# Base product of an adaptive FFN layer with LoRA experts: Strassen's seven block products over pairs of rows, in two passes over the contraction

## The reference

```python
y      = einsum('bct,bcd->bdt', x, w_cond[idx])         # 128x128 matrix per row, picked by idx
base   = einsum('bnd,od->bno', y, W_base) + b_base      # W_base 2048 x 2048
probs  = softmax(einsum('bnd,ed->bne', y, W_gate))      # 8 experts
route  = weights of the two largest probs, divided by their sum
h      = einsum('bnd,erd->bner', y, A)                  # 8 experts x rank 16 = 128 features
delta  = einsum('bner,eor->bno', h * route, B)
out    = x + base + delta * 1.0
```

## Time and profile before

| | |
|---|---|
| time, median of 3 runs | 1686.07 us (1685.47 to 1686.70) |
| the profiled execution | 1686.61 us, its span 1684.7 us |
| busy share of the span | PE 98%, DVE 49%, ACT 15%, POOL 13% |
| mean granted TensorE clock | 0.992 of 2.4 GHz |
| DRAM traffic | 89.49 MB, mean 53 GB/s; 228 GB/s in the first of 40 slices |
| 128x512 matmuls | 5952 of the base product, 384 of the expert part |

### The profile page before, as it was taken

How to read it: one execution, slowest core, us unless ns; L and a number is a source line. 1 busy time by engine, 2 the same in 40 slices (tenths; PEclk the granted TensorE clock), 3 DMA queues, 4 the chain that set the end, 5 groups by cost and what they waited for, 6 DMA issues and landing times.

```text
span 1684.7 us, 27043 instructions
## 1 busy us (share of the span) xinstructions
PE 1645.8 (98%) x10563; PEld 893.3 (53%) x10563; DVE 827.8 (49%) x1801; ACT 247.7 (15%) x416; POOL 223.6 (13%) x132
## 2 busy tenths in 40 slices
PE   5899999999999999999999999999999999999998
PEld 5785555455555455555545555554555554555553
DVE  5866554444545454454445444545445444544452
ACT  5661111001011101011110101110001111010110
POOL 2652111100111110111111011111011111101110
PEclk8999999999999999999999999999999999999999
DMA  6341110111110111111011111101111101111100
GB/s 228 126 177 59 46 52 19 51 45 45 51 45 28 42 51 45 45 45 51 24 46 45 45 51 45 39 31 51 45 45 51 45 25 45 45 51 45 45 25 25
DMA packets 32111, 89.49 MB, mean 53 GB/s; under 512 B 3386, under 2 KB 8506, under 8 KB 25946
## 3 DMA queue, kind: packets, MB, share of 16 engines
q1 hardware_dynamic: 32090, 89.21, 14.5%
HBM read 55.64 MB, written 33.55 MB: 53 GB/s over the span
## 4 chain that ended last, share of the span: by engine, by line
PE 95%; DVE 2%; issue 1%; ACT 1%; DMA 0%; SPq 0%; DVEq 0%; POOL 0%; ACTq 0%; POOLq 0%
PE acc L732 26%; PE acc L731 26%; PE acc L733 26%; PE h_ps L733 2%; PE h_ps L731 2%; PE h_ps L732 2%; PE tr L731 2%; PE delta L731 2%; PE tr L732 2%; PE tr L733 2%; PE delta L733 2%; PE delta L732 2%; PE tr L784 1%; DVE WT L504 0%; DMA x_even<-in_x_dram 0%
## 5 line engine op out<-in xcount | busy, mean ns | idle before, releaser
L732 PE MATMUL acc<-WT,y_parts 128*128 128x512 f16 (+2 forms) x2240 | 799.6, 361 | 0.0
L731 PE MATMUL acc<-WT,y_parts 128*128 128x512 f16 (+2 forms) x2240 | 799.3, 361 | 0.0
L733 PE MATMUL acc<-WT,y_parts 128*128 128x512 f16 (+2 forms) x2240 | 799.3, 361 | 0.0
L733 PEld LDWEIGHTS acc<-WT,y_parts 128*128 128x128 f16 x2240 | 219.8, 98 | 234.1
L731 PEld LDWEIGHTS acc<-WT,y_parts 128*128 128x128 f16 x2240 | 219.8, 98 | 219.1
L732 PEld LDWEIGHTS acc<-WT,y_parts 128*128 128x128 f16 x2240 | 219.8, 98 | 217.8
L504 DVE SCALAR_TENSOR_TENSOR y_parts<-tr,y_parts 128x512 f16<-128x512 f32 x126 | 86.9, 691 | 238.3 <-ACT y_parts L352 237.7
L592 DVE SCALAR_TENSOR_TENSOR scaled_acc<-acc,y_inv,inv_w 128x512 f32<-128x512 f32 x128 | 95.8, 749 | 189.2 <-PE delta L733 182.8
L352 ACT ACTIVATE y_parts<-tr 128x512 f16<-128x512 f32 x126 | 75.1, 597 | 502.0 <-PE tr L733 501.9
L299 POOL TENSOR_TENSOR wait_taker<-amax,ident 128x2 f32<-128x2 f32 x32 | 6.3, 197 | 947.4 <-DVE amax L483 947.4
L476 DVE TENSOR_SCALAR clamped<-amax_all 128x2 f32<-128x2 f32 x32 | 5.4, 170 | 210.9 <-POOL amax_all L300 210.9
(11 more groups left out here) (175 smaller groups left out, 1393.5 us busy)
## 6 DMA issues: line engine op xcount, KB each, us to landing
x_even<-in_x_dram SPq DMA_DIRECT2D x16, 1024.0 KB, 4.8
x_odd<-in_x_dram SPq DMA_DIRECT2D x16, 1024.0 KB, 4.8
out_dram<-x_even SPq DMA_DIRECT2D x64, 256.0 KB, 2.5
out_dram<-x_odd SPq DMA_DIRECT2D x64, 256.0 KB, 2.5
x_odd<-in_L_ffn_W_base_dram SPq DMA_DIRECT2D x4, 1024.0 KB, 5.0
bias<-in_L_ffn_W_base_dram SPq DMA_DIRECT2D x4, 1024.0 KB, 4.8
spare<-in_L_ffn_W_base_dram SPq DMA_DIRECT2D x4, 1024.0 KB, 4.9
x_parts<-in_L_ffn_W_base_dram SPq DMA_DIRECT2D x3, 1024.0 KB, 4.7
```

The lines of the kernel that those rows point to most:

```text
L731: nc.tensor.matmul(dst, lhs[0], rhs[0], start=start, stop=False)
L732: nc.tensor.matmul(dst, lhs[0], rhs[1], start=False, stop=False)
L733: return nc.tensor.matmul(dst, lhs[1], rhs[0], start=False, stop=stop)
```

## The change

Rows are taken in pairs. With A the outputs of `cond` for the two rows (two rows by two halves of a piece of the contraction) and B the matching blocks of `W_base` (two halves of the contraction piece by two blocks of 512 outputs), four blocks of the result of 128x512 are made from seven block products in place of eight. Sums of A (S1 to S4), of B (T1 to T4) and of the results are needed for it.

- **Two passes.** The contraction of 2048 is cut into two halves of 1024. Steps 0 to 15 (first pass) take the 16 pairs over the first half, steps 16 to 31 over the second. A step makes 8 tiles of 128x512 (j or c and s below: two rows by four groups of outputs). The first pass adds residual and bias and stores each tile to `part_dram`; the second loads it again, adds its own half and the expert part, and stores to `out`.
- **W twice.** `TT` holds the seven B-combinations of one half, split (112 KB of each partition). It is built before step 0 and again, for the other half, between steps 15 and 16, each time in 8 units of two 128x1024 blocks of rows.
- **Features.** `make_features` sums into `BH` in each step; the first pass stores its half of h to `h_dram`, the second adds it. Routing and expert part are done in the second pass only, for both rows together.
- **Results.** ACT copies the partial products that are needed twice (`copy_p`), DVE makes tile and row scale (`finish`), POOL adds it to the residual tile (`add_r`), and in the first pass the bias (`add_bias`).
- The loops are written out; nothing of row 0 is made inside the preparation of W.

TensorE and the sums around it:

```diff
+    def product(n, s, q):
+        if s == 0:
+            pe.wait_ge(s_lo, n_s(n, q))
...
+        elif q == 5:
+            pe.wait_ge(p_copied, n_copy(n, s, P5_COPY))
+        elif q == 6:
+            pe.wait_ge(p_copied, n_copy(n, s, U2_COPY))
+        dst = (BX[s], BY[1], BY[0], BX[s], BZ, BY[1], BX[s])[q]
+        for c in range(C4):
+            mm = three(dst[:, :], [SO[:, slot(n, q), part, c, :] for part in range(2)],
+                       [TT[:, q, s, part, c, :] for part in range(2)],
+                       opens and c == 0, c == C4 - 1, q not in (2, 4))
+        mm.then_inc(prod_done, 1)
...
+    for n in range(NSTEP):
+        product(n, 0, 0)
+        make_features(n)
+        for q in range(1, NPROD):
+            product(n, 0, q)
+            if q == 4 and second:
+                transpose_hw(n)
+            if q == 5 and more:
+                cond(n + 1, U_A11)
+            if q == 6:
+                if more:
+                    cond(n + 1, U_S1)
+                if second:
+                    delta(n, 0)
+        for q in range(NPROD):
+            product(n, 1, q)
+            if q < 2 and more:
+                cond(n + 1, (U_A12, U_A22)[q])
+            if second and q < 6:
+                delta(n, q + 1)
+                if q == 5:
+                    delta(n, 7)
```

POOL in a step, and one unit of W on POOL:

```diff
+    def add_bias(m):
+        _, o = tile_of(m % 8)
+        pool.wait_ge(xr_in[xr_slot(m)], xr_turn(m))
+        link(nc.gpsimd.tensor_tensor(XR[:, xr_slot(m), :], XR[:, xr_slot(m), :], bias[:, o:o + Q], ALU.add))
+    def add_r(m):
...
+        pool.wait_ge(r_ready, m + 1)
+        nc.gpsimd.tensor_tensor(XR[:, xr_slot(m), :], XR[:, xr_slot(m), :], TM[:, m % 2, :],
+                                ALU.add).then_inc(r_added, 1)
+    for n in range(NSTEP):
+        if n + 1 < NSTEP:
+            share_maxima(n + 1)
+        if n < NP:
+            add_bias(8 * n)
+            for j in range(8):
+                if j < 7:
+                    add_bias(8 * n + j + 1)
+                add_r(8 * n + j)
+        else:
+            for j in range(8):
+                add_r(8 * n + j)
...
+    def w_lower(g):
+        for i, q in enumerate((T1, T3, T2, T4)):
+            pool.wait_ge(w_sum_hi, 4 * g + i + 1)
+            nc.gpsimd.tensor_tensor(t_dst(q, u, 1), quads(t_full[q]), t_dst(q, u, 0), ALU.subtract)
```

DVE in a step (of `finish`, the waits and the two instructions; `s_lower` and the sums `sum_s2`, `sum_s4_s3` are one `tensor_tensor` of 128x512 each, from SBUF and SBUF), and the rebuild between the passes:

```diff
+            def finish(n, s, c):
+                m = 8 * n + 4 * s + c
+                src, at, q, copy, op = ((BY[0], 0, 2, P1_COPY, ALU.add), (BY[1], 0, 5, U2_COPY, ALU.add),
+                                        (BX[s], 2, 6, P4_COPY, ALU.subtract), (BX[s], 1, 6, P5_COPY, ALU.add))[c]
+                _, o = tile_of(m % 8)
+                dve.wait_ge(prod_done, n_prod(n, s, q))
+                dve.wait_ge(p_copied, n_copy(n, s, copy))
+                if m >= 2:
+                    dve.wait_ge(r_added, m - 1)
+                nc.vector.scalar_tensor_tensor(out=TM[:, m % 2, :], in0=src[:, :],
+                                               scalar=y_inv[:, n % 2, c // 2:c // 2 + 1],
+                                               in1=PC[:, at, :], op0=ALU.mult, op1=op).then_inc(t_done, 1)
+                dve.wait_ge(t_done, m + 1)
+                nc.vector.tensor_tensor(TM[:, m % 2, :], TM[:, m % 2, :], inv_w[:, o:o + Q],
+                                        ALU.mult).then_inc(r_ready, 1)
...
+            for n in range(NSTEP):
+                more, second = n + 1 < NSTEP, n >= NP
+                if more:
+                    find_maxima(n + 1)
+                features(n)
+                if second:
+                    route_tokens(n)
+                    weigh_features(n)
+                finish(n, 0, C11)
+                if more:
+                    scale_x(n + 1)
+                if second:
+                    split_hwT_lo(n)
+                if more:
+                    split_x_lo(n + 1, 0)
+                    split_x_lo(n + 1, 1)
+                finish(n, 0, C12)
...
+                finish(n, 0, C21)
+                finish(n, 0, C22)
...
+                if more:
+                    s_lower(n + 1, A11)
+                    s_lower(n + 1, S1)
...
+                if more:
+                    sum_s2(n + 1)
+                    s_lower(n + 1, A12)
...
+                finish(n, 1, C11)
+                if more:
+                    s_lower(n + 1, S2)
...
+                if more:
+                    sum_s4_s3(n + 1)
+                    s_lower(n + 1, A22)
...
+                if more:
+                    s_lower(n + 1, S4)
+                    s_lower(n + 1, S3)
+                finish(n, 1, C12)
...
+                finish(n, 1, C21)
+                finish(n, 1, C22)
+                if n == NP - 1:
+                    dve.wait_ge(r_added, 8 * NP)
+                    w_scales(NU)
+                    for g in range(NU, 2 * NU):
+                        if g + 1 < 2 * NU:
+                            w_scales(g + 1)
+                        w_sums_and_lower(g)
```

More of the change, by code:

```diff
@@ L138, in adaln_ffn_kernel @@
[L138 to L153, removed]
@@ L777, in transpose_group @@
-            def transpose_group(rows, scales, used, j):
-                pe.wait_ge(*used)
-                for c in range(GK):
-                    dst, chunk = ring[j][:, c * P:(c + 1) * P], rows[:, j, c * P:(c + 1) * P]
-                    if scales is None:
-                        mm = nc.tensor.transpose(dst, chunk, ident[:, :])
-                    else:
-                        mm = nc.tensor.matmul(dst, chunk, diag[:, scales, :], start=True, stop=True)
-                mm.then_inc(tr_filled, 1)
@@ L892, in _, with three @@
-            with pe.Fori(1, NB - 1) as b:
-                period(b)
-            period(NB - 1, last=True)
+            def three(dst, lhs, rhs, start, stop, chained=False):
+                nc.tensor.matmul(dst, lhs[0], rhs[0], start=start, stop=False, skip_group_check=chained)
+                nc.tensor.matmul(dst, lhs[0], rhs[1], start=False, stop=False, skip_group_check=chained)
+                return nc.tensor.matmul(dst, lhs[1], rhs[0], start=False, stop=stop, skip_group_check=chained)
@@ new lines, in cond @@
+            def cond(n, u):
+                i, half = ((0, 0), (1, 0), (0, 1), (1, 1))[u]
+                pe.wait_ge(xp_lo, 2 * n + 1 + i)
+                if n > 0 or u > 0:
+                    pe.wait_ge(af_copied, 4 * n + u)
+                for c in range(C4):
+                    ts = slice(half * Q + c * P, half * Q + (c + 1) * P)
+                    mm = three(BC[:, c * P:(c + 1) * P], [XP[:, s, i, ts] for s in range(2)],
+                               [WCP[:, s, i, :] for s in range(2)], True, True)
+                mm.then_inc(cond_done, 1)
@@ new lines, in _ @@
+            pe.wait_ge(consts, E + 2)
+            w_quads(0)
+            pe.wait_ge(agb_diag, 2)
+            nc.tensor.matmul(BC[:, 0:P], ones[:, :], agb_diag_inv[:, 0:P], start=True, stop=True)
+            nc.tensor.matmul(BC[:, P:P + E], ones[0:E, :], agb_diag_inv[0:E, P:P + E],
+                             start=True, stop=True).then_inc(agb_spread, 1)
+            w_quads(1)
+            for j in range(4):
+                if j > 0:
+                    pe.wait_ge(a_copied, j)
+                for c in range(C4):
+                    ts = slice(j * Q + c * P, j * Q + (c + 1) * P)
+                    mm = nc.tensor.matmul(BD[:, c * P:(c + 1) * P], a_staged[:, ts], agb_diag_f, start=True, stop=True)
+                mm.then_inc(a_tr, 1)
```

1466 lines of the change are left out of this document (835 added, 631 removed).

## The result

The changed kernel takes **1715.28 us** (median of 4 runs, 1709.94 to 1717.43) against 1686.38 for the kernel before on the same chip: a ratio of 1.0164, 95% interval 1.0139 to 1.019. It is slower by 29 us, or 1.6%. The forecast was 1704, slower, with a range of 1645 to 1745. The profiled execution took 1715.63, with a span of 1713.5.

What follows compares the result with a forecast made beforehand. TensorE, busy 98%, was taken to bound the kernel before. Start 130 + first pass 722 + rebuild 74 + second pass 773 − 3 + tail 6 = 1702 span, plus 1.9 around it: 1704 us, range 1645 to 1745.

Steps and rivals of the forecast that it cites:

- The sign and the sum: Whole kernel: Strassen takes away 167 us of matmuls, but unhidden preparation of W and waits make it slower, 1704 us.
- Start, "130": Before the first product: building W's parts with A, gate, B and first x between takes 130 us, bounds 115 to 150.
- Preparation of W, "74": Between the passes: rebuilding the weight parts in 8 units of 8.2 us stands alone and takes 74 us.
- While both add, they take turns.: DVE and POOL two-input SBUF instructions lock each other out in the first pass: 12 x 1.1 + 11 x 0.55 us.
- The step by hand: First-pass step followed across engines: POOL can add from 20.1 us, last sum done at 40.5, last product at 42.5.
- The stall of 3.4 before the last product: First pass: TensorE waits 3.4 us a step for ACT's copy U2, queued behind S3's upper part.
- 45.1 us a step: First-pass step: 41.74 us of matmuls plus the stall, 722 us for the pass; bounds 41.74 and 47.0.
- Rival 3: First-pass stalls lower TensorE's clock, losing about 1.9 us per step: 1734 us; chance 0.1.
- The second pass: Steps of 48.3 us, 773 in all: matmuls 47.14 plus a 1.1 us wait for x at `cond`; bounds 47.1 and 51.
- Rival 1: First pass: POOL does not break queued DVE runs, U2 is in time, POOL's circle bounds: 43.5 a step, 1678 us; chance 0.2.
- Rival 2: First pass: POOL never waits for DVE, nothing is late, steps take 41.74 us: 1650 us; chance 0.14.
- Rival 4: Second pass: routing makes the transposition late, 3 us a step, 16 times: 1752 us; chance 0.09.

Runs made afterwards that it cites:

- experiment 2: Changed kernel with the first pass's bias additions moved from GpSimd (POOL) to VectorE (DVE), nothing left out: 1648.7 us, ratio 0.978 to the kernel before.
- experiment 6: Changed kernel without rebuilding the transformed weights between the passes, the second pass reusing the first half's: 1646.43 us, ratio 0.9764 to the kernel before.
- experiment 8: Changed kernel with bias on VectorE and, in the second pass, the next step's x scaled and split earlier: 1634.81 us, ratio 0.9697 to the kernel before.
- experiment 7: Changed kernel plus eight useless 512-column products ahead of the even-to-odd row's last product in the first pass: 1712.76 us, ratio 1.0157 to the kernel before.
- experiment 5: Changed kernel with each first-pass bias addition on GpSimd replaced by four zero fills that read no SBUF: 1652.47 us, ratio 0.98 to the kernel before.

## Why the prediction was right, and where it was off

- **The sign and the sum.** 167 us of matmuls saved, and more than that given back in three places, as forecast: the start and the rebuilding, which row work no longer hides, and the stall of the first pass. Experiments 2 and 6 show the last two by themselves: 1715.3 − 1648.7 = 67 us for the stall with its clock, 69.9 us for the rebuilding. Of the 196 us given back (167 + 29) these leave 59 for the start, the second pass's waits, the rest of the border and the tail; experiment 8 won back 14 of them (1648.7 − 1634.8).
- **Start, "130".** 125.4, inside its bounds; a sum of many estimates, 4.6 too high, which hid part of the first pass's miss.
- **Preparation of W, "74".** 73.9, but not for just its reasons. A unit took 7.85 (in the timeline of PE the diagonals' matmuls begin at 902.26 and 910.11), forecast 8.2. ACT waited 8.7 us there for W's loads from DRAM, which the forecast did not have.
- **"While both add, they take turns."** Shown: 1.68 us for one of each, forecast 1.1 + 0.55 = 1.65. DVE's lateness and POOL's are both in the rows. The rule cited, the Trainium skill, "SBUF — State Buffer" (the lock is held for a whole instruction and blocks the other fully), agrees with the trace in the main: 1.75 and 1.71 us side by side, 0.69 and 1.26 alone. One of each takes 1.68, less than 0.69 + 1.26 = 1.95, so a part of 0.27 us of their lone times does overlap.
- **The step by hand.** In the step shown, counted from the end of the product before it (402.14), GpSimd's first addition starts at 20.3 (forecast 20.1), the last sum ends at 41.0 (40.5), and the last product starts at 42.3 (42.5). So this was no luck.
- **The stall of 3.4 before the last product.** 3.15 on average, at the place named and through the copy named; swinging between 1.7 and 4.25 from step to step. Why it swings is open.
- **The failed step: "45.1 us a step".** It added no clock to its own stall. The fall of the clock was priced (1.9 us), but as a rival that happens in every step or in none. It happened in 8 of 15, 1.7 us each. The sum of the first pass: 16 x 41.74 = 668, waits 47.3 + 3.05 in the last step = 50.4 (forecast 54), falls 15, slow first matmuls 1.5, about 3 unassigned: 737.8. Rival 3 was half of the case: the measured waits alone would have made the pass 4 us shorter than forecast, not 15.8 longer.
- **The second pass.** The wait for x is 0.8 a step, forecast 1.1. Experiment 8, by taking it away, gained 0.96.
- **Rival 1, DVE keeps its turn: excluded.** The sums in a run, 439.67 and 441.36, each wait for one instruction of POOL. (Its price was misadded: 13.3 + 13 x 1.23 + 9 + 4.6 is 42.9, not 43.5, which would be 35 us less, not 26.)
- **Rival 2, POOL never waits: excluded.** Its biases take 1.441 on average against 1.26, 1.71 where DVE has work.
- **Rival 4, routing late: excluded.** Features, routing and weighting ran from 1041.30 to 1048.94, 7.6 us (forecast 8.4), and TensorE never waited for them.

## What to carry to other kernels

When a faster matmul scheme hands its savings to VectorE and GpSimd, count their two-operand SBUF additions as one shared resource: beside each other one of each took 1.68 us, so an addition moved to VectorE (0.68 us) could cost less than the same one on GpSimd. A stall forecast on TensorE needs the price of the clock behind it added in proportion, not put aside as a separate case. And look for the whole circle: here halving the turns, or giving back GpSimd's 14 us for the shared maxima, each removed the stall, while reordering one queue moved part of it to the next wait.

## What the runs showed of the hardware that was not expected

- The granted clock fell after only some waits of nearly the same length: in the changed kernel after 2.96 us and not after 3.58; in experiment 7, with the useless products between the product before and the wait, after 1.96 and not after 2.15. Each fall of ordinary length cost 1.7 us.
- GpSimd's fills of 128x256 did not lengthen VectorE's two-operand additions at all (0.68 to 0.69 us, 94 of them), while its own additions of 128x512 brought them to 1.75.
- The idle behind the all-reduce (7.63 us, where the earlier trace rows had 6.99) stands ahead of the next addition, not of the next instruction. In experiment 5 (timeline of POOL) the fills start at 391.10, right behind the all-reduce of 390.84, and the 7.22 us of idle come behind them, before the addition at 401.29.
